# Softmax in an attention layer: the maxima subtracted on VectorE, one exponential for four heads on ScalarE

## The chip, the cores and the metric

The kernel runs on one core of a Trainium2 chip. The metric is the device time of one execution in microseconds (us). The engines are TensorE (PE in the profile, PEld for its weight loads), VectorE (DVE), ScalarE (ACT), GpSimd (POOL) and SyncE (SP).

## What is computed

Two layers, each an attention over a context of 128 rows and a mixture of eight experts, on 32 batches of 128 rows of 256 numbers:

```python
x = x + jnp.tanh(g_xattn[0]) * _L0_xattn_ref(_layernorm(x), ctx_1024, ctx_1024, ...)
x = x + jnp.tanh(g_ffn[0]) * _L0_ffn_ref(_layernorm(x), ...)
x = x + jnp.tanh(g_xattn[1]) * _L1_xattn_ref(_layernorm(x), ctx_1024, ctx_1024, mask, ...)
x = x + jnp.tanh(g_ffn[1]) * _L1_ffn_ref(_layernorm(x), ...)
```

The attention has 16 heads of 16 numbers; the second layer adds a mask to the scores:

```python
scores = jnp.einsum('bhqd,bhkd->bhqk', q, k) / jnp.sqrt(jnp.float32(D_K))
attn = jax.nn.softmax(scores, axis=-1)
out = jnp.einsum('bhqk,bhkd->bhqd', attn, v)
```

## The kernel before, in words

Each layer has an attention stage and an expert stage, one after the other. The change lies in the attention stages.

An attention stage works through 128 **units**: a batch and four of its heads, so four units per batch. The order is written out by hand. Every engine runs one loop over **steps** s, and in step s does its part of the units and batches that are due then; what is due when stands in the loop as an offset. Engines wait for each other by counters only (`w.wait_ge`), and each works through its own list in order. Sixteen steps are four batches, a **group**; the work for a group (layer norm, transposes of its rows, query, key and value projections, and the routing of an earlier group's rows to the experts) is spread over the 16 steps, so steps differ. Steps are named here by their place in the 16.

A unit i goes through these places:
- TensorE, step i - 4: scores of 128 query rows by 4 heads x 128 keys, into one of three PSUM banks (`SB_[i % 3]`, `ps0` to `ps2`), by three matmuls (lines 420 to 422; in the second layer a fourth, line 518, adds the mask). The query weights are scaled negatively, so the scores are negated and the largest weight belongs to the minimum.
- VectorE, step i - 3: the minimum of each head's 128 scores (line 1153) into `mx`. It is the first thing that VectorE does in a step.
- ScalarE, step i - 2: exp(minimum - score), one activation for each head, since the bias is one number per row and head (line 743), from the bank into one of three buffers of weights, `PB[:, i % 3]` (in `U`, `U3` with its number).
- TensorE, step i: four transposes of `PB` (line 500, counter `m_t`), into one of two banks `PTB` (`ps3`, `ps4`), which the transposes of the outputs (line 525) take turns with. It is the first thing that TensorE does in a step; the scores of unit i + 4 follow.
- ScalarE, step i: a copy of the transposed weights into `PT` (line 750). TensorE then multiplies them with the values (line 488), two units at a time, in the even steps.

Every fourth step (3, 7, 11, 15) VectorE goes on behind the reduction with the reciprocal (line 1157) and the normalisation (line 1163) of the batch whose outputs TensorE transposed a step earlier. The transposes of the next step (line 500 in steps 4, 8, 12, 0) need the bank that line 1163 reads. Behind that, VectorE has the low parts of projected rows (lines 916, 922 or 924, 932 or 934), statistics (1079, 1083, 1227, 1231), layer norm (1093, steps 4 and 5, for TensorE's transposes, line 435, in steps 6 and 7), and the routing's small operations. Line 916 in step 8 is what the query projection of that step waits for.

TensorE in step s may write the scores of unit s + 4 when the bank's unit s + 1 is done with.

Of the kernel before, what the change touches and what calls it, by code (L numbers as in the profile page):

```python
# [10 lines left out]
ACT = mybir.ActivationFunctionType  # L11
ALU = mybir.AluOpType
AX = mybir.AxisListType
# [133 lines left out]
def program(nc, A):  # L147
    ctx = ExitStack()
    with ctx:  # L149
# [3 lines left out]
        def mark(name, keys, step=1):  # L153
            return Mark(ctx.enter_context(nc.semaphore(name)), keys, step)
# [38 lines left out]
        mx = sb("mx", [128, 4, 4])  # L193
# [40 lines left out]
        PB = U3[:, 0:1536].rearrange("p (r h k) -> p r h k", r=3, h=4)  # L234
# [9 lines left out]
        SB_, PTB, OB, BK, BO_, HBK, YB, XB = PS[0:3], PS[3:5], PS[5], PS[6], PS[7], PS[0:4], PS[4:6], PS[6:8]  # L244
# [8 lines left out]
        units = [(L, i) for L in LL for i in range(NU)]  # L253
# [35 lines left out]
        m_s, m_t, m_av = (mark(n, units) for n in ("m_s", "m_t", "m_av"))  # L289
# [1 line left out]
        m_o, a_o = mark("m_o", bats), mark("a_o", bats)  # L291
        m_ot, m_op = mark("m_ot", range(B)), mark("m_op", range(B))
        m_lt, m_lg, m_rk = mark("m_lt", prt2), mark("m_lg", prts), mark("m_rk", prts)
        v_mx, a_p, a_pt = (mark(n, units) for n in ("v_mx", "a_p", "a_pt"))
        a_xt, v_xt, a_q, v_q, a_k, v_k, a_v = (mark(n, gt2) for n in ("a_xt", "v_xt", "a_q", "v_q", "a_k", "v_k", "a_v"))
        a_ct, v_st1 = (mark(n, grps) for n in ("a_ct", "v_st1"))
        p_ct, v_ct = mark("p_ct", [k for k in grps if k[1]]), mark("v_ct", [(0, 0), (1, 0)])
# [194 lines left out]
        def pe_attention(e, w, L):  # L492
            pe_first(e, w, L)
            for s in range(FIRST, LAST):
                if 0 <= s < NU:
                    i, bank = s, pt_place["p", s]
                    w.wait_ge(*a_p[L, i])
                    turn_free(w, L, "p", i)
                    for h in range(4):
                        ins = e.transpose(bank[:, h * 128:(h + 1) * 128], PB[:, i % 3, h], ident)  # L500
                    ins.then_inc(*m_t(L, i))
                if 0 <= s + 4 < NU:
                    i = s + 4
                    b, m, z = i // 4, (i // 2) % 2, i % 2
                    g, j, bank = b // G, b % G, SB_[i % 3]
                    w.wait_ge(*v_q[L, g, 1])
                    if i < 2:
                        w.wait_ge(*a_v[L, 0, i])
                    w.wait_ge(*d_k[key_queue(L, b)][L, b, 7])
                    if i >= 3:  # L510
                        w.wait_ge(*a_p[L, i - 3])
                    js = slice(j * 128, j * 128 + 128)
                    kh, kl = (KX[:, b % 2, p, m, 4 * z:4 * z + 4, :].rearrange("p h k -> p (h k)") for p in range(2))
                    ins = three(e, bank[:, :], (QR[:, g % 2, 0, m, js], QR[:, g % 2, 1, m, js]), (kh, kl), True, L == 0)
                    if L == 1:
                        w.wait_ge(*v_mk[g])
                        w.wait_ge(*s_ir[0])
                        ins = e.matmul(bank[:, :], IR[:, :], MK[:, g % 2, j:j + 1, :].to_broadcast([128, 4, 128]), start=False, stop=True)
                    ins.then_inc(*m_s(L, i))
# [209 lines left out]
        def act_attention(e, w, L):  # L729
            act_first(e, w, L)  # L730
            for s in range(FIRST, LAST):
                if (b := bat(s, OC)) is not None:
                    w.wait_ge(*m_av[L, 4 * b + 3])
                    if b:
                        w.wait_ge(*m_o[L, b - 1])
                    e.activation(OS[:, :], OB[:, :], ACT.Copy).then_inc(*a_o(L, b))
                if 0 <= s + 2 < NU:
                    i = s + 2
                    w.wait_ge(*v_mx[L, i])
                    if i >= 3:  # L740
                        w.wait_ge(*m_t[L, i - 3])
                    for h in range(4):
                        ins = e.activation(PB[:, i % 3, h], SB_[i % 3][:, h * 128:(h + 1) * 128], ACT.Exp, bias=mx[:, i % 4, h:h + 1], scale=-1.0)  # L743
                    ins.then_inc(*a_p(L, i))
                if 0 <= s < NU:
                    i = s
                    w.wait_ge(*m_t[L, i])
                    if i >= 3:
                        w.wait_ge(*m_av[L, i - 3])
                    e.activation(PT[:, i % 3].rearrange("p h k -> p (h k)"), pt_place["p", i][:, :], ACT.Copy).then_inc(*a_pt(L, i))  # L750
                if (g := grp(s, -2)) is not None:
                    act_context(e, w, L, g)
                for at, take in ((X0, act_turn), (Q0, act_query), (K0, act_key), (V0, act_value)):
                    for n in range(2):
                        if (g := grp(s, at[n])) is not None:
                            take(e, w, L, g, n)
                if L == 0 and (b := bat(s, 8)) is not None:
                    w.wait_ge(*m_ot[b])
                    if b >= 2:
                        w.wait_ge(*m_op[b - 2])  # L760
                    e.activation(OT[:, b % 2, 0].rearrange("p t n -> p (t n)"), place[0, "ot", b][:, 0:256], ACT.Copy).then_inc(*a_ot(b))
                for p in PARTS:
                    k, g, js = (L,) + p.key, p.g, p.js
                    for t in range(2):
                        if s == p.lt[t]:
                            cs = slice(p.lo * 128, p.hi * 128)
                            w.wait_ge(*m_lt[k + (t,)])
                            if p.lo == 0 and g:
                                w.wait_ge(*m_lg[L, g - 1, 0])
                            e.activation(LT[:, t, cs], place[L, "lt", p.key, t][:, cs], ACT.Copy).then_inc(*a_lt(*k, t))  # L770
                    if s == p.lt[1]:
                        w.wait_ge(*v_xr[k])
                        if p.lo == 0 and 0 < g < NG - 1:
                            w.wait_ge(*d_sc[(g - 1) % 2][L, g - 1, 0, 1, G - 1])
                        e.activation(xr(g)[:, 1, js, 0:D], xr(g)[:, 0, js, 0:D], ACT.Copy).then_inc(*a_xr(*k))
                    if s == p.exp:
                        if L == 0:
                            w.wait_ge(*v_ga1[k])
                            e.activation(rt[:, 1, js, 0], rt[:, 0, js, 0], ACT.Exp).then_inc(*a_gx(*k))
                        else:  # L780
                            w.wait_ge(*v_ga1[k])
                            e.activation(rt[:, 3, js], rt[:, 1, js], ACT.Exp)
                            e.activation(rt[:, 6, js], rt[:, 4, js], ACT.Exp).then_inc(*a_gx(*k))
# [361 lines left out]
        def dve_attention(e, w, L):  # L1145
            dve_first(e, w, L)
            for s in range(FIRST, LAST):
                if 0 <= s + 3 < NU:
                    i = s + 3
                    w.wait_ge(*m_s[L, i])  # L1150
                    if i >= 4:
                        w.wait_ge(*a_p[L, i - 4])
                    e.tensor_reduce(mx[:, i % 4], SB_[i % 3][:, :].rearrange("p (h k) -> p h k", h=4), AX.X, ALU.min).then_inc(*v_mx(L, i))  # L1153
                if (b := bat(s, 7)) is not None:
                    w.wait_ge(*m_o[L, b])
                    o = pt_place["o", b][:, :].rearrange("p (h d) -> p h d", d=32)
# [512 lines left out]
```

## Time and profile before

| | us |
|---|---|
| median of 3 runs | 1687.52 |
| lowest, highest | 1686.19, 1691.3 |
| the profiled execution, first to last instruction (span) | 1689.9 |
| attention of the first layer, first to last reduction | 27.5 to 358.5 |
| attention of the second layer | 916.3 to 1259.3 |

The page prints the span of the profiled execution and no other time of it. A row of busy time by stretch gives, for each engine, the microseconds in which it executed something; a row of waits gives who sat idle until whom. Engine time that is not busy can be a wait for another engine, or the short gap between two dependent operations on the same engine.

### The profile page before, as it was taken

How to read it: one execution, taken by the hardware profiler on the slowest of the kernel's cores; microseconds unless marked ns; L12 is line 12 of the kernel's file. 1: busy time of each engine (PE TensorE's matmuls, PEld its weight loads, DVE VectorE, ACT ScalarE, POOL GpSimd, SP SyncE). 2: the span in 40 equal slices, each digit the busy share in tenths (PEclk: the TensorE clock that was granted, in tenths of full speed). 3: DMA queues.
4: the chain of work that ended last, by engine and by line, in shares of the span. 5: the costliest groups of instructions: out<-in, count | busy, mean ns of one | idle time of the engine just before them, and what ended most of it. 6: DMA issues, size and time to landing. Idle time of an engine off the chain costs nothing. (4 is left out here: it accounts for less than half of the span.)

```text
span 1689.9 us, 37219 instructions
## 1 busy us (share of the span) xinstructions
PE 1575.0 (93%) x12832; PEld 1424.2 (84%) x12832; DVE 1194.5 (71%) x2829; ACT 1232.1 (73%) x2859; POOL 826.4 (49%) x887
## 2 busy tenths in 40 slices
PE   7999999976999999999988999999984999999996
PEld 5788888865999999999986777777773899999996
DVE  5677777755777777777766788888857566766664
ACT  5888888853888888888863877777771577777774
POOL 3224444343556565656552113333323477777776
PEclk9999999987999999999998999999995999999999
DMA  3222222135877777778742223333232788788883
GB/s 110 54 50 75 75 76 76 51 95 148 261 235 235 224 230 228 232 226 236 225 141 78 72 82 104 107 104 104 62 90 77 200 225 242 222 230 231 226 233 99
DMA packets 208988, 256.56 MB, mean 152 GB/s; under 512 B 29555, under 2 KB 156788, under 8 KB 208800
## 3 DMA queue, kind: packets, MB, share of 16 engines
q1 hardware_dynamic: 185408, 217.95, 44.2%
q0 software_dynamic: 21120, 34.39, 7.9%
q10 hardware_dynamic: 2272, 1.85, 0.4%
q8 instruction: 102, 1.67, 0.4%
q14 instruction: 86, 0.70, 0.1%
HBM read 194.54 MB, written 45.74 MB: 142 GB/s over the span
## 5 line engine op out<-in xcount | busy, mean ns | idle before, releaser
L1276 POOL TENSOR_TENSOR KXR<-U,KXR 128x1024 fp32r<-128x1024 f32 (+1 forms) x156 | 355.2, 2277 | 276.9 <-ACT KXR L795 276.9
L420 PE MATMUL ps<-QR,KXR 128*128 128x256 f32 x1248 | 360.4, 289 | 0.8 <-DVE QR L1280 0.7
L422 PE MATMUL ps<-QR,KXR 128*128 128x256 f32 x1248 | 354.2, 284 | 0.0
L421 PE MATMUL ps<-QR,KXR 128*128 128x256 f32 x1248 | 354.0, 284 | 0.0
L795 ACT ACTIVATE KXR<-U 128x1024 fp32r<-128x1024 f32 (+1 forms) x312 | 287.4, 947 | 73.2 <-PE ps L422 49.4
L743 ACT ACTIVATE U<-ps,mx 128x128 f32<-128x128 f32 x1024 | 299.0, 405 | 20.3 <-DVE mx L1153 20.3
L420 PEld LDWEIGHTS ps<-QR,KXR 128*128 128x128 f32 x1248 | 240.6, 193 | 1.4 <-DVE QR L1280 1.3
L421 PEld LDWEIGHTS ps<-QR,KXR 128*128 128x128 f32 x1248 | 240.4, 193 | 0.0
L422 PEld LDWEIGHTS ps<-QR,KXR 128*128 128x128 f32 x1248 | 240.0, 192 | 0.0
L1153 DVE TENSOR_REDUCE mx<-ps 128x4 f32<-128x512 f32 x256 | 174.3, 684 | 69.3 <-PE ps L422 37.1
L1276 DVE TENSOR_TENSOR KXR<-U,KXR 128x1024 fp32r<-128x1024 f32 (+1 forms) x156 | 175.0, 1160 | 25.6 <-ACT KXR L795 25.5
L1403 POOL DMA_INDIRECT xs_scr<-XR,PI x112 | 109.8, 980 | 133.6 <-DVE PI L1060 104.6
L500 PE MATMUL ps<-cst,U 128*128 128x128 f32 x1024 | 163.5, 283 | 10.0 <-DVE U L1163 9.5
L750 ACT ACTIVATE U<-ps 128x512 f32<-128x512 f32 x256 | 166.5, 650 | 7.4 <-PE ps L500 7.4
L500 PEld LDWEIGHTS ps<-cst,U 128*128 128x128 f32 x1024 | 117.3, 143 | 48.1 <-issue 23.6
L821 ACT ACTIVATE U<-ps,b1s 128x256 f32<-128x256 f32 x312 | 130.4, 473 | 29.9 <-PE ps L422 29.9
L1307 DVE TENSOR_TENSOR PTR<-U,PTR 128x512 fp32r<-128x512 f32 x80 | 101.0, 1298 | 60.6 <-ACT PTR L832 60.6
L420 PE MATMUL ps<-KXR,PTR 128*128 128x256 f32 x480 | 136.1, 284 | 3.6 <-ACT U L810 1.5
L1307 DVE TENSOR_TENSOR WR<-U,WR 128x512 fp32r<-128x512 f32 x76 | 97.9, 1326 | 56.6 <-ACT WR L832 56.6
L421 PE MATMUL ps<-KXR,PTR 128*128 128x256 f32 x480 | 135.8, 283 | 0.0
L422 PE MATMUL ps<-KXR,PTR 128*128 128x256 f32 x480 | 135.8, 283 | 0.0
L1419 POOL DMA_INDIRECT out<-U,xi x78 | 121.1, 1552 | 20.0 <-issue 19.7
(206 smaller groups left out, 4043.3 us busy)
## 6 DMA issues: line engine op xcount, KB each, us to landing
U<-in_wpack SPq DMA_DIRECT2D x234, 512.0 KB, 4.4
U<-in_wpack SPq DMA_DIRECT2D x78, 256.0 KB, 4.2
KXR<-U SPq DMA_DIRECT2D x504, 32.0 KB
U<-xs_scr SPq DMA_DIRECT2D x39, 258.0 KB, 4.5
U<-xs_scr SPq DMA_DIRECT2D x39, 257.0 KB, 4.7
U<-in_ctx_t SPq DMA_DIRECT2D x16, 512.0 KB, 5.7
U<-ys_scr SPq DMA_DIRECT2D x32, 256.0 KB, 3.4
XR<-in_L_ffn_b SPq DMA_DIRECT2D x39, 128.0 KB, 3.9
```

The source lines that it names most:

```text
L420: e.matmul(o, wh, xh, start=first, stop=False)
L421: e.matmul(o, wh, xl, start=False, stop=False)
L422: return e.matmul(o, wl, xh, start=False, stop=done)
L500: ins = e.transpose(bank[:, h * 128:(h + 1) * 128], PB[:, i % 3, h], ident)
L743: ins = e.activation(PB[:, i % 3, h], SB_[i % 3][:, h * 128:(h + 1) * 128], ACT.Exp, bias=mx[:, i % 4, h:h + 1], scale=-1.0)
L750: e.activation(PT[:, i % 3].rearrange("p h k -> p (h k)"), pt_place["p", i][:, :], ACT.Copy).then_inc(*a_pt(L, i))
L795: e.activation(w_cols(L, WH, n), w_raw(L, n), ACT.Copy).then_inc(*a_w[n](L, i))
L821: ins = e.activation(HB[:, r, f], HBK[q][:, z * 256:z * 256 + 256], ACT.Relu, bias=b1s[:, r, f:f + 1])
L1153: e.tensor_reduce(mx[:, i % 4], SB_[i % 3][:, :].rearrange("p (h k) -> p h k", h=4), AX.X, ALU.min).then_inc(*v_mx(L, i))
L1276: e.tensor_tensor(w_cols(L, WL, n), w_raw(L, n), hi, ALU.subtract).then_inc(*l_w[n](L, i))
L1307: ins = e.tensor_tensor(low[:, 2 * q:2 * q + 2], HB[:, i % 2, 2 * q:2 * q + 2], high[:, 2 * q:2 * q + 2], ALU.subtract)
L1419: ins = e.indirect_dma_start(ys_d[1], at, yo[:, r, a, :], None, bounds_check=T - 1, oob_is_err=False, compute_op=ALU.add)
```

## The change

VectorE gets a second operation behind each reduction: minimum - score for all four heads, 128x512, from the bank into the buffer of weights, the minima read with a step of zero over 128 columns. ScalarE then takes the exponential of the buffer in place, in one activation without a bias from memory. A new counter, `v_sb`, tells that the subtraction is done: ScalarE waits for it, and so does TensorE before it writes new scores into the bank. The wait for the buffer to be free (`m_t` of the unit three back) moves from ScalarE to VectorE, which also waits for its own reduction (`v_mx`) and no longer for the exponential four units back.

```diff
@@ pe_attention
                     if i >= 3:
-                        w.wait_ge(*a_p[L, i - 3])
+                        w.wait_ge(*v_sb[L, i - 3])
@@ act_attention
                     i = s + 2
-                    w.wait_ge(*v_mx[L, i])
-                    if i >= 3:
-                        w.wait_ge(*m_t[L, i - 3])
-                    for h in range(4):
-                        ins = e.activation(PB[:, i % 3, h], SB_[i % 3][:, h * 128:(h + 1) * 128], ACT.Exp, bias=mx[:, i % 4, h:h + 1], scale=-1.0)
-                    ins.then_inc(*a_p(L, i))
+                    w.wait_ge(*v_sb[L, i])
+                    flat = PB[:, i % 3].rearrange("p h k -> p (h k)")
+                    e.activation(flat, flat, ACT.Exp).then_inc(*a_p(L, i))
@@ dve_attention
                     w.wait_ge(*m_s[L, i])
-                    if i >= 4:
-                        w.wait_ge(*a_p[L, i - 4])
-                    e.tensor_reduce(mx[:, i % 4], SB_[i % 3][:, :].rearrange("p (h k) -> p h k", h=4), AX.X, ALU.min).then_inc(*v_mx(L, i))
+                    scores = SB_[i % 3][:, :].rearrange("p (h k) -> p h k", h=4)
+                    e.tensor_reduce(mx[:, i % 4], scores, AX.X, ALU.min).then_inc(*v_mx(L, i))
+                    if i >= 3:
+                        w.wait_ge(*m_t[L, i - 3])
+                    w.wait_ge(*v_mx[L, i])
+                    e.tensor_tensor(PB[:, i % 3], mx[:, i % 4, :, None].to_broadcast([128, 4, 128]), scores, ALU.subtract).then_inc(*v_sb(L, i))
```

Line numbers shift by up to three; line 1153 is the reduction before and the subtraction after.

VectorE in the first layer, step 3 of a middle group, before (the names in brackets are the counters that an operation waits for):

```order
L993 TENSOR_TENSOR rt<-m8 128x4
L1153 TENSOR_REDUCE mx<-ps1 128x4 [waits a_p,m_s]
L1157 RECIPROCAL rec<-ps3 128x16 [waits m_o]
L1163 TENSOR_TENSOR U4<-ps3,rec 128x256 [waits m_ot,v_c]
L950 SCALAR_TENSOR_TENSOR X<-ps7,th,X 128x256 [waits p_xb,m_op]
L965 COPY RK<-ps6 128x64 [waits m_rk]
```

And after:

```order
L990 TENSOR_TENSOR rt<-m8 128x4
L1149 TENSOR_REDUCE mx<-ps1 128x4 [waits m_s]
L1153 TENSOR_TENSOR U3<-mx,ps1 128x512 [waits v_mx,m_t]
L1157 RECIPROCAL rec<-ps3 128x16 [waits m_o]
L1163 TENSOR_TENSOR U4<-ps3,rec 128x256 [waits m_ot,v_c]
L947 SCALAR_TENSOR_TENSOR X<-ps7,th,X 128x256 [waits p_xb,m_op]
L962 COPY RK<-ps6 128x64 [waits m_rk]
```

The subtraction stands between the reduction and the normalisation, with a wait for this step's transposes.

VectorE in the second layer, steps 5 to 7 of a middle group, before:

```order
L1153 TENSOR_REDUCE mx<-ps1 128x4 [waits a_p,m_s]
L1093 TENSOR_SCALAR U2<-X,mv,rs 128x256 x2
L1153 TENSOR_REDUCE mx<-ps2 128x4 [waits a_p,m_s]
L1102 TENSOR_TENSOR MK<-U3,cst 128x512 [waits p_mf]
L1153 TENSOR_REDUCE mx<-ps0 128x4 [waits a_p,m_s]
L1157 RECIPROCAL rec<-ps4 128x16 [waits m_o]
L1163 TENSOR_TENSOR U4<-ps4,rec 128x256 [waits v_c]
L1167 SCALAR_TENSOR_TENSOR X<-U4,th,X 128x256 [waits v_on]
L916 TENSOR_TENSOR PTR<-ps6,PTR 128x512 [waits a_xt]
```

And after:

```order
L1149 TENSOR_REDUCE mx<-ps1 128x4 [waits m_s]
L1153 TENSOR_TENSOR U3<-mx,ps1 128x512 [waits v_mx,m_t]
L1090 TENSOR_SCALAR U2<-X,mv,rs 128x256 x2
L1149 TENSOR_REDUCE mx<-ps2 128x4 [waits m_s]
L1153 TENSOR_TENSOR U3<-mx,ps2 128x512 [waits v_mx,m_t]
L1099 TENSOR_TENSOR MK<-U3,cst 128x512 [waits p_mf]
L1149 TENSOR_REDUCE mx<-ps0 128x4 [waits m_s]
L1153 TENSOR_TENSOR U3<-mx,ps0 128x512 [waits v_mx,m_t]
L1157 RECIPROCAL rec<-ps4 128x16 [waits m_o]
L1163 TENSOR_TENSOR U4<-ps4,rec 128x256 [waits v_c]
L1167 SCALAR_TENSOR_TENSOR X<-U4,th,X 128x256 [waits v_on]
L913 TENSOR_TENSOR PTR<-ps6,PTR 128x512 [waits a_xt]
```

Three operations are added in a stretch of nine rows; the rest keeps its order.

ScalarE in the first layer, steps 8 and 9 of a group, before:

```order
L743 ACTIVATE U3<-ps0,mx 128x128 [waits v_mx]
L743 ACTIVATE U3<-ps0,mx 128x128 x3
L750 ACTIVATE U3<-ps4 128x512 [waits m_av,m_t]
L668 ACTIVATE QR<-ps7,bqk 128x512 [waits m_s,m_q]
L761 ACTIVATE OT<-ps6 128x256 [waits m_op,m_ot]
L736 ACTIVATE OS<-ps5 128x512 [waits m_o,m_av]
```

And after:

```order
L741 ACTIVATE U3<-U3 128x512 [waits v_sb]
L747 ACTIVATE U3<-ps4 128x512 [waits m_av,m_t]
L668 ACTIVATE QR<-ps7,bqk 128x512 [waits m_s,m_q]
L758 ACTIVATE OT<-ps6 128x256 [waits m_op,m_ot]
L736 ACTIVATE OS<-ps5 128x512 [waits m_o,m_av]
```

Four activations from the bank become one within the buffer.

## Rows read from the trace of the kernel before

**Rows 1.** The page's first section: busy us, share of the span, instructions.
```profile
PE 1575.0 (93%) x12832; PEld 1424.2 (84%) x12832; DVE 1194.5 (71%) x2829; ACT 1232.1 (73%) x2859; POOL 826.4 (49%) x887
```

**Rows 2.** Busy time by stretch: start:end, length, then each engine; the two stages.
```profile
core 0: us, PE busy (x) PEld busy (x) DVE busy (x) ACT busy (x) POOL busy (x), PEclk, DMA share, GB/s
27.46:358.50 331.04, 320.81 (x2795) 260.94 (x2793) 231.47 (x698) 275.64 (x781) 121.03 (x265) 1.00 0.26 70
916.26:1259.30 343.04, 323.37 (x2678) 255.81 (x2676) 275.15 (x818) 263.95 (x755) 105.21 (x242) 0.98 0.32 91
```

**Rows 3.** The same for one middle group of each layer, cut into stretches.
```profile
191.10:206.37 15.27, 15.27 (x138) 12.68 (x137) 10.08 (x38) 13.92 (x38) 3.06 (x2) 1.00 0.15 31
206.37:219.35 12.98, 12.52 (x120) 10.06 (x119) 11.90 (x41) 11.60 (x35) 7.50 (x18) 1.00 0.29 79
219.35:234.50 15.15, 14.78 (x121) 12.35 (x119) 9.52 (x24) 10.67 (x30) 7.68 (x20) 1.00 0.39 114
...
1085.75:1116.90 31.15, 28.71 (x229) 22.65 (x228) 29.70 (x100) 23.87 (x69) 10.64 (x20) 0.95 0.18 48
1117.00:1132.03 15.03, 15.03 (x130) 12.23 (x129) 9.06 (x22) 10.67 (x31) 5.44 (x17) 1.00 0.69 202
```

**Rows 4.** Timeline, second layer: start, length, engine, line, operation, idle before and releaser.
```profile
1103.25 0.68 DVE L1153 TENSOR_REDUCE mx<-ps 128x4 f32<-128x512 f32 x1
1103.85 0.25 DVE L1157 RECIPROCAL rec<-ps 128x16 f32<-128x16 f32 x1
1104.13 0.42 DVE L1163 TENSOR_TENSOR U<-ps,rec 128x256 f32<-128x256 f32 x1
...
1104.61 0.66 PE L500 MATMUL ps<-cst,U 128*128 128x128 f32 x4 [1.91 <-DVE U L1163]
```

**Rows 5.** Timeline, first layer, around steps 3 to 8 of one group.
```profile
209.07 0.42 DVE L1163 TENSOR_TENSOR U<-ps,rec 128x256 f32<-128x256 f32 x1
...
209.25 0.66 PE L500 MATMUL ps<-cst,U 128*128 128x128 f32 x4
...
216.12 0.63 PE L435 MATMUL ps<-cst,U 128*128 128x128 f32 x4 [0.44 <-DVE U L1093]
...
221.26 0.47 PE L420 MATMUL ps<-PTR,WR 128*128 128x512 f32 x1 [0.37 <-DVE PTR L916]
```

**Rows 6.** Groups by line and shape: count, busy us, mean ns, idle before.
```profile
L916 DVE TENSOR_TENSOR PTR<-ps,PTR 128x512 fp32r<-128x512 f32 x32 | 21.8, 685 | 6.1 <-ACT PTR L659 6.0
L1163 DVE TENSOR_TENSOR U<-ps,rec 128x256 f32<-128x256 f32 x64 | 27.2, 425 | 2.2
L922 DVE SCALAR_TENSOR_TENSOR QR<-ps,bqk,QR 128x512 fp32r<-128x512 f32 x16 | 12.0, 751 | 23.9 <-ACT QR L668 23.9
L1102 DVE TENSOR_TENSOR MK<-U,cst 128x512 fp32r<-128x512 f32 x8 | 5.4, 681 | 0.0
...
L736 ACT ACTIVATE OS<-ps 128x512 f32<-128x512 f32 x64 | 38.9, 609 | 9.0 <-PE ps L488 8.9
```

**Rows 7.** Busy time of line 1153 alone (VectorE) in the two full stretches.
```profile
206.37:219.35 12.98, 4.01 (x6) 1.00 0.29 79
1085.75:1116.90 31.15, 7.48 (x11) 0.95 0.18 48
```

**Rows 8.** Line 743: its group on the page, and who waited for it.
```profile
L743 ACT ACTIVATE U<-ps,mx 128x128 f32<-128x128 f32 x1024 | 299.0, 405 | 20.3 <-DVE mx L1153 20.3
...
  PEld ps L420: 7.0, 15
  PE ps L420: 3.8, 7
```

**Rows 9.** Busy time of TensorE and its granted clock (third number) by stretch.
```profile
1105.60:1108.40 2.80, 2.80 (x23) 0.50 0.21 42
```

**Rows 10.** Timeline of VectorE and GpSimd, second layer, step 15.
```profile
1089.56 2.60 DVE L1072 SCALAR_TENSOR_TENSOR X<-U,GT,X 128x256 f32<-128x256 f32 x1
...
1089.45 2.43 POOL L1351 TENSOR_TENSOR PTR<-U,PTR 128x1024 fp32r<-128x1024 f32 x1 [6.75 <-ACT PTR L653]
```

More of the change, by code:

```diff
@@ L293, in program @@
         m_lt, m_lg, m_rk = mark("m_lt", prt2), mark("m_lg", prts), mark("m_rk", prts)
-        v_mx, a_p, a_pt = (mark(n, units) for n in ("v_mx", "a_p", "a_pt"))
+        v_mx, v_sb, a_p, a_pt = (mark(n, units) for n in ("v_mx", "v_sb", "a_p", "a_pt"))
         a_xt, v_xt, a_q, v_q, a_k, v_k, a_v = (mark(n, gt2) for n in ("a_xt", "v_xt", "a_q", "v_q", "a_k", "v_k", "a_v"))
```

## The prediction

> **What bounds the kernel now.** I read five views, from the whole to the place. The page's first section gives the share of each engine in the span: TensorE 93%, VectorE 71%, ScalarE 73% [rows 1]. The change touches only the two attention stages, so I next read the busy time stage by stage. In the first layer's stage (331.04 us) TensorE is busy for 320.81, VectorE for 231.47, ScalarE for 275.64; in the second layer's (343.04 us) it is 323.37, 275.15 and 263.95 [rows 2]. Read as averages, TensorE is the bound and VectorE has 30% and 20% to spare. One group of 16 steps from the middle of each stage tells more. In the first layer VectorE is busy 11.90 of the 12.98 us from step 2 to step 7 and only 10.08 of 15.27 and 9.52 of 15.15 on either side. In the second it is busy 29.70 of the 31.15 us from step 14 to step 8 of the next round, and 9.06 of the other 15.03 [rows 3]. What is missing in the full stretches are gaps of some hundredths of a microsecond between dependent small operations, and at most one short wait. So VectorE is not an engine with 25% to spare: it is full for a third of each group in the first layer and for two thirds in the second, and idle in the rest, where the query, key and value projections keep TensorE busy without a break.
>
> The waits say that TensorE already feels the full stretches. In the second layer its transposes wait 1.91 us for line 1163, VectorE's normalisation one step earlier [rows 4]. In the first layer it waits 0.44 us for line 1093 (layer norm) and 0.37 us for line 916 (low part of the turned rows), both at the end of the full stretch [rows 5]. These are small, but they show that no slack is left between the two engines there: what makes VectorE later at these places makes TensorE later.
>
> **The price of a subtraction.** The trace has no instruction just like the new one: 128x512, scores from PSUM, four maxima each spread over 128 columns, result to SBUF. Line 916 is a TENSOR_TENSOR of the same size with one input in PSUM (685 ns), line 1163 one with a spread operand (425 ns for 256 columns), line 922 a heavier form (751 ns) [rows 6]. The nearest is 0.685. In the queue, a 0.68 us reduction that is followed by independent work holds VectorE for 0.60 (1103.25 to 1103.85); a dependent operation starts 0.03 after the end of the one before it (line 1157, 0.25 long, 1103.85; line 1163 at 1104.13) [rows 4]. So reduction and subtraction hold it for 0.68 + 0.03 + about 0.61 = 1.32 where the reduction held it for 0.60: **0.72 us per unit**. Bounds: 0.60, if the dependence costs nothing; 0.79, if the subtraction lasts as long as line 922. A gain is excluded here, since the reduction stays.
> The Trainium skill (Perfetto Trace Analysis, Optimizing Scalar/DVE Operations) puts the overhead of a VectorE operation that reads PSUM at about 125 ns, against about 60 ns for SBUF. By it 512 columns would cost an estimated 0.66 us, and 123 of them 81 us. The rows do not bear the difference out: line 1102 reads SBUF and takes 681 ns, line 916 reads PSUM and takes 685 [rows 6].
>
> **Part by part.** (1) *VectorE gets 256 subtractions*, 184 us at 0.72. Those in stretches where it idles cost nothing: there each group has 10 steps (first layer) or 5 (second), thus 7.2 and 3.6 us, against 10.8 and 6.0 us of idle time in the same rows [rows 3]. TensorE's projections hide them, and without this cover they would cost 0.72 each. Those in full stretches lie on the path: 6 reductions stand in the first layer's and 11 in the second's [rows 7]. I take five middle groups of each layer at the full count, 5 x (6 + 11) = 85, and the other three of each, the first two and the last, which lack part of the routing work that fills VectorE, at three quarters, 38: together 123. **123 x 0.72 = 89 us.** With 0.60 and 0.79 it is 74 and 97.
> (2) *VectorE gets a wait* before the subtraction, for the transposes of the unit three back, which TensorE does at the start of the same step. Queued behind it are, every fourth step, lines 1157 and 1163, for which the next transposes wait, and the low parts that the projections need. Where TensorE runs ahead it costs nothing, and a late VectorE lets it run ahead. The place where it is not: in the first layer TensorE transposes at 209.25 to 209.91, and line 1163 follows VectorE's reduction at 209.07 [rows 5]. After the change the subtraction can't start before 209.91 and line 1163 ends 0.68 + 0.03 + 0.25 + 0.03 + 0.42 later, at 211.3. By the count of subtractions alone it would be 209.49 + 2 x 0.72 = 210.9. The wait's 0.4 us is made up where TensorE must wait for line 1093 in any case; I take nothing, and 0.4 x 8 = 3 us for the range.
> (3) *ScalarE loses* four activations per unit, 299.0 us in 256 units, 1.17 us each, and gets one of 128x512, for which line 736 takes 609 ns [rows 6, 8]: some 0.56 us less per unit, 144 us in all. On the path there is little of it: all that TensorE waited for line 743, weight loads and matmuls together, is 10.8 us [rows 8]. I count nothing.
> (4) *The score bank is free earlier*: TensorE's next scores wait for the subtraction, no longer for the exponential behind it. That wait is within the same 10.8 us. The removed wait of the reduction (for the exponential four units back) never shows. TensorE's own list is unchanged.
>
> **The sum.** 1689.9 (span) + 89 = 1779. The page prints the span and not the time around it; the median of the runs is 2.4 below that span, so on its scale I predict 1687.5 + 89 = **1777 us**.
>
> **Rivals.**
> *A: the averages decide.* Three score banks and three weight buffers might let VectorE fall behind in the full stretch and catch up in the idle one. Then a group needs only its total. First layer: 11.5 + 31.5 = 43.0 in 43.4 us, no change. Second: 11.5 + 38.8 = 50.3 against 46.2, 4.1 us in five groups: 1687.5 + 21 = 1708. Against it stand the waits without slack [rows 4, 5]: line 1163 lies between TensorE's steps every fourth step, and banks don't help there. Chance 0.09.
> [...]
> *B: the clock.* In the second layer, after the 1.91 us in which TensorE did nothing, its granted clock reads 0.50 (1.2 GHz of its 2.4) for the 2.80 us from 1105.60 [rows 9], so 1.4 us of work at the full clock took twice that. The change makes several stalls of 1 to 4 us per group. If each group loses one such 1.4 us more on the path, 16 groups lose 22: 1687.5 + 89 + 22 = 1799. It decides if TensorE, once released, is what VectorE or the next projection waits for. In the second layer VectorE stays the later one, which speaks against it; the first layer's projections follow right behind its stalls, which speaks for it. Chance 0.15.
> *C: not slower.* ScalarE's relief is what counts: TensorE's waits for line 743 vanish (10.8 us), and the subtractions hide as the stage averages suggest: 1687.5 - 11 = 1677. It needs the full stretches to be waits in disguise, with VectorE held up by others. Within them rows 3 leave 1.1 and 1.5 us for all gaps and waits, which is against it. Chance 0.03.
> That the change doesn't do what it says is out: the order shows one subtraction behind each reduction and one activation for four.
>
> **How the numbers follow.** The forecast has 0.70; A 0.09, B 0.15, C 0.03, and 0.03 is left for more than all this. One term can go either way: once per group of the second layer line 1072 lasts 2.60 us beside GpSimd's line 1351 instead of about 0.48 [rows 10]; a shifted start can lose that overlap or add one, 2.1 us in 7 groups, 15 us. Low end: 74 - 15 - 4 of slack that I may have missed, 1687.5 + 55 = 1742. High end: 97 + 22 + 3 + half of 15, 1687.5 + 129 = 1816. It takes in B and leaves A, C and the rest out. A measurement of this kernel can tell about 0.3% (5 us) from no change. Faster by more: 0.03 (C); within: 0.03 (between C and A); slower: 0.94.
>
> **What would show it.** In the profile after: the subtraction at 0.68 to 0.70 us; VectorE about 184 us busier, ScalarE about 140 less; the first layer's stage some 31 us longer and the second's some 57; TensorE's waits for lines 1163, 1093 and 916 up from a dozen to tens of microseconds; the projections' stretches (from 219.35 and from 1117.0) as long as before. If the stages grow by 0 and 20, A is right; if the granted clock of the stages falls well below the 1.00 and 0.98 of rows 2 and the projections' stretches grow, B. I am wrong in the main if TensorE's waits for VectorE stay as they are while VectorE is busier, or if subtractions last well over 0.8 us.

## The result and the profile after

| | before | after |
|---|---|---|
| median of 4 runs each (us) | 1688.5 | 1837.9 |
| lowest, highest | 1686.2, 1691.3 | 1836.1, 1840.9 |
| span of the profiled execution | 1689.9 | 1835.1 |
| first layer's attention, first to last reduction | 330.3 | 409.4 |
| second layer's attention, first to last reduction | 343.9 | 413.3 |
| from the first layer's last reduction to the second's first | 556.9 | 557.2 |

The changed kernel takes 1.0885 times as long, interval [1.0863, 1.0906]: 149 us more. The prediction said slower, by 89, with 1816 as the upper end of the range; the time lies 22 us above that end and 61 above the forecast. All but a microsecond of it is in the two attention stages, 79 us in the first layer and 69 in the second. The stages are measured here from the start of the first reduction to the start of the last. (The second layer's first reduction starts at 914.7 us in the kernel before, not at 916.3 as in the table ahead of the prediction; nothing above hangs on it.)

The first section of the page after (busy us, share of the span, instructions) against [rows 1]:

```profile
PE 1617.9 (88%) x12832; PEld 1445.4 (79%) x12832; DVE 1354.9 (74%) x3085; ACT 1117.1 (61%) x2091; POOL 826.7 (45%) x887
```

VectorE is 160 us busier and ScalarE 115 less. The groups by line (count, busy us and mean ns of one, then the idle time of the engine before them and who ended it), against [rows 6, 8]. Line 1153 is now the subtraction, 1149 the reduction, 741 the exponential:

```profile
L1153 DVE TENSOR_TENSOR U<-mx,ps 128x512 f32<-128x512 f32 x256 | 176.1, 688 | 137.5 <-PE ps L500 120.5 <-DVE mx L1149 1.1
L1149 DVE TENSOR_REDUCE mx<-ps 128x4 f32<-128x512 f32 x256 | 172.5, 674 | 1.6 <-PE ps L518 1.3 <-PE ps L422 0.3
L500 PE MATMUL ps<-cst,U 128*128 128x128 f32 x1024 | 170.8, 292 | 53.9 <-ACT U L741 46.9 <-DVE U L1163 5.9 <-ACT U L747 1.0
L741 ACT ACTIVATE U<-U 128x512 f32<-128x512 f32 x256 | 160.4, 627 | 78.6 <-DVE U L1153 75.8
```

The subtraction takes 688 ns and the exponential of four heads 627 ns, as foreseen. Unforeseen is the first row's idle time: VectorE sat 120.5 us in front of the subtraction, waiting for the transposes of line 500. The waits (engine, what it was about to write, line, for whom: total us, times, longest):

```profile
DVE U L1153 <- PE ps L500: 120.5, 97, 2.9
...
PE ps L435 <- DVE U L1090: 32.5, 14, 4.4
...
PE ps L420 <- DVE PTR L913: 19.5, 16, 1.7
```

The first row is VectorE in front of the subtraction, 97 times. The exponential comes behind the subtraction: ScalarE waits for it 75.8 us (the fourth row of the groups), and TensorE's transposes wait for the exponential 46.9 (the third row). Before, TensorE's transposes hardly waited for ScalarE's exponentials at all (0.4 us of line 500's weight loads in the whole run). Lines 1090 and 913 are the layer norm and the low part that were lines 1093 and 916. TensorE waits for them 32.5 and 19.5 us, against 9.2 and 7.0 before. The prediction named line 1163 first; the transposes now wait for it 5.9 us in all (the third row of the groups).

Busy time by stretch, columns as in [rows 2]: the two stages, and the same pieces of a middle group as in [rows 3], cut at the same units' reductions:

```profile
26.30:436.40 410.10, 344.63 (x2795) 269.62 (x2793) 312.48 (x824) 218.73 (x400) 120.71 (x265) 0.95 0.21 56
992.90:1406.80 413.90, 347.44 (x2684) 271.52 (x2682) 355.68 (x946) 208.01 (x376) 106.83 (x242) 0.93 0.27 75
```

```profile
226.90:244.60 17.70, 15.77 (x116) 12.41 (x116) 12.88 (x45) 10.18 (x18) 3.10 (x3) 0.90 0.10 21
244.60:264.79 20.19, 14.33 (x118) 10.54 (x117) 16.87 (x47) 8.79 (x17) 10.47 (x21) 0.92 0.27 80
264.79:282.97 18.18, 16.67 (x143) 13.52 (x142) 12.39 (x29) 10.12 (x20) 4.64 (x17) 1.00 0.25 67
1202.08:1241.58 39.50, 29.30 (x220) 22.71 (x219) 36.91 (x112) 17.89 (x33) 13.47 (x22) 0.91 0.18 49
1241.58:1258.07 16.49, 16.49 (x140) 13.56 (x139) 11.77 (x27) 9.72 (x18) 3.09 (x15) 1.00 0.56 158
```

The first layer's pieces were 15.27, 12.98 and 15.15 us and are now 17.70, 20.19 and 18.18: the full stretch grew by 7.2, and the two pieces of projections, in which VectorE idles, grew by 2.4 and 3.0. In the second layer the full stretch (31.15) grew by 8.4 and the other (15.03) by 1.5. The subtractions alone were to lengthen the full stretches, and only those. In two of the three pieces with idle time the granted clock is 1.00, as before, so in these the clock is not what made them longer.

The timeline shows how a stretch with idle time grows. The end of step 8 and step 9 of a middle group, first layer, VectorE and TensorE (start, length, engine, line, operation, idle before it and releaser):

```profile
266.28 0.68 DVE L913 TENSOR_TENSOR PTR<-ps,PTR 128x512 fp32r<-128x512 f32 x1
...
267.11 0.47 PE L420 MATMUL ps<-PTR,WR 128*128 128x512 f32 x1 [0.77 <-DVE PTR L913]
...
267.43 0.66 DVE L1149 TENSOR_REDUCE mx<-ps 128x4 f32<-128x512 f32 x1
...
269.46 0.66 PE L500 MATMUL ps<-cst,U 128*128 128x128 f32 x4
...
270.15 0.69 DVE L1153 TENSOR_TENSOR U<-mx,ps 128x512 f32<-128x512 f32 x1 [2.06 <-PE ps L500]
...
270.76 0.74 DVE L919 SCALAR_TENSOR_TENSOR QR<-ps,bqk,QR 128x512 fp32r<-128x512 f32 x1
...
271.56 0.50 PE L420 MATMUL ps<-PTR,WR 128*128 128x512 f32 x1 [0.74 <-DVE QR L919]
```

VectorE ends step 9's reduction at 268.09 (267.43 + 0.66) and then stands for 2.06 us: its next operation, the subtraction, needs the transposes at 269.46, and TensorE does those behind the projection that began at 267.11 and behind the values' product. Line 919, the low part of the projected rows, is queued behind the subtraction, and the next projection (271.56) waits for line 919. Projection, transposes, subtraction, low part, next projection: one after the other. From projection to projection it takes 4.45 us (271.56 - 267.11). The same step before, where the low part is line 922:

```profile
223.61 0.66 PE L500 MATMUL ps<-cst,U 128*128 128x128 f32 x4
223.64 0.75 DVE L922 SCALAR_TENSOR_TENSOR QR<-ps,bqk,QR 128x512 fp32r<-128x512 f32 x1 [1.39 <-ACT QR L668]
...
224.80 0.39 PE L420 MATMUL ps<-PTR,WR 128*128 128x512 f32 x1
```

There the low part runs beside the transposes, the projection doesn't wait, and from the projection at 221.26 [rows 5] to this one it is 3.54 us.

### The profile page after: what moved, and what is told of

It is laid out like the page before. It is cut to its first block and busy times, and to the rows that moved or that the text cites. A ratio compares the mean times of both kernels' runs of the same rounds, so it can differ in the third digit from the quotient of the medians.

```text
span 1835.1 us, 36893 instructions
## 1 busy us (share of the span) xinstructions
PE 1617.9 (88%) x12832; PEld 1445.4 (79%) x12832; DVE 1354.9 (74%) x3085; ACT 1117.1 (61%) x2091; POOL 826.7 (45%) x887
## 5 line engine op out<-in xcount | busy, mean ns | idle before, releaser
L1153 DVE TENSOR_TENSOR U<-mx,ps 128x512 f32<-128x512 f32 x256 | 176.1, 688 | 137.5 <-PE ps L500 120.5
L500 PE MATMUL ps<-cst,U 128*128 128x128 f32 x1024 | 170.8, 292 | 53.9 <-ACT U L741 46.9
L741 ACT ACTIVATE U<-U 128x512 f32<-128x512 f32 x256 | 160.4, 627 | 78.6 <-DVE U L1153 75.8
L1276 DVE TENSOR_TENSOR KXR<-U,KXR 128x1024 fp32r<-128x1024 f32 (+1 forms) x156 | 177.4, 1175 | 26.1 <-ACT KXR L792 26.0
L747 ACT ACTIVATE U<-ps 128x512 f32<-128x512 f32 x256 | 151.4, 591 | 66.6 <-PE ps L500 66.2
```

Source lines behind the costliest of these rows:

```text
L741: e.activation(flat, flat, ACT.Exp).then_inc(*a_p(L, i))
L1153: e.tensor_tensor(PB[:, i % 3], mx[:, i % 4, :, None].to_broadcast([128, 4, 128]), scores, ALU.subtract).then_inc(*v_sb(L, i))
L1276: e.tensor_tensor(w_cols(L, WL, n), w_raw(L, n), hi, ALU.subtract).then_inc(*l_w[n](L, i))
```

## The experiments

Two theories stood against each other for the missing 61 us. **W**: it is the wait that moved into VectorE's list, which the prediction took at nothing. **V**: the wait is a symptom; the added work of VectorE costs that much more than 0.72 us a subtraction, in the full stretches or in the others too. The clock (rival B of the prediction) stood beside them. All ratios are against the kernel before, run beside them.

**The wait taken away (e1_four).** A fourth buffer of weights; the subtraction then waits for transposes that TensorE did a step earlier. To make room for it, the second layer's mask is computed in place, and the load of the next mask waits for a later operation; e2_work, e6_idle and e8_full share this. e6_idle comes out within 3.5 us of the kernel before, so it costs little. The rest is as in the changed kernel.

```diff
...
+        P4 = U3[:, 3584:4096].rearrange("p (h k) -> p h k", h=4)
+        PBS = [PB[:, 0], PB[:, 1], PB[:, 2], P4]
...
-                    if i >= 3:
-                        w.wait_ge(*m_t[L, i - 3])
+                    if i >= 4:
+                        w.wait_ge(*m_t[L, i - 4])
                     w.wait_ge(*v_mx[L, i])
-                    e.tensor_tensor(PB[:, i % 3], mx[:, i % 4, :, None].to_broadcast([128, 4, 128]), scores, ALU.subtract).then_inc(*v_sb(L, i))
+                    e.tensor_tensor(PBS[i % 4], mx[:, i % 4, :, None].to_broadcast([128, 4, 128]), scores, ALU.subtract).then_inc(*v_sb(L, i))
...
```

> The changed kernel with a fourth buffer of weights (the second layer's mask is computed in place to make room), so that the subtraction waits for the transposes of the unit four back, which TensorE did a step earlier. Theory W (the wait that moved into VectorE's queue costs what the prediction missed, about 60 of the 150 us, because in the steps with a projection it ties each VectorE step to the end of TensorE's step before): 1777 us, 1765 to 1790, and VectorE's wait before the subtraction falls from 120 us to under 30. Theory V (the work of the subtraction alone costs 150 us, since hardly any of it finds idle time): 1830 to 1840.

Measured: 1775.45 us, 1.0516 [1.0499, 1.0533]: 87 us over the kernel before and 62 under the changed one. The group of the subtraction (line 1155 here; lines are two further down) no longer names a releaser:

```profile
L1155 DVE TENSOR_TENSOR U<-mx,ps 128x512 f32<-128x512 f32 x256 | 176.0, 688 | 26.1
```

The 26.1 us over 256 of them are 0.10 each, the gap behind the reduction that it depends on. The same step as above, TensorE and VectorE:

```profile
245.28 0.47 PE L422 MATMUL ps<-PTR,WR 128*128 128x512 f32 x1 [0.39 <-DVE PTR L915]
...
245.60 0.66 DVE L1151 TENSOR_REDUCE mx<-ps 128x4 f32<-128x512 f32 x1
...
246.36 0.69 DVE L1155 TENSOR_TENSOR U<-mx,ps 128x512 f32<-128x512 f32 x1
...
247.63 0.66 PE L502 MATMUL ps<-cst,U 128*128 128x128 f32 x4
247.66 0.75 DVE L921 SCALAR_TENSOR_TENSOR QR<-ps,bqk,QR 128x512 fp32r<-128x512 f32 x1 [0.62 <-ACT QR L670]
...
248.83 0.40 PE L422 MATMUL ps<-PTR,WR 128*128 128x512 f32 x1
```

The subtraction (246.36) now runs while TensorE projects, the low part (line 921, 247.66) runs beside the transposes (line 502), and from projection to projection it takes 248.83 - 245.28 = 3.55 us instead of 4.45. By pieces of a middle group:

```profile
208.24:223.29 15.05, 15.05 (x138) 12.65 (x136) 13.28 (x44) 11.23 (x21) 3.11 (x3) 1.00 0.15 31
223.29:243.05 19.76, 15.51 (x120) 11.97 (x119) 17.11 (x48) 8.83 (x17) 10.57 (x21) 0.84 0.26 81
243.05:258.59 15.54, 15.15 (x121) 12.65 (x119) 12.75 (x29) 8.63 (x17) 4.55 (x17) 0.99 0.26 74
1152.41:1189.95 37.54, 29.63 (x228) 23.04 (x227) 34.94 (x113) 18.68 (x34) 13.38 (x22) 0.91 0.20 53
1189.95:1205.22 15.27, 15.27 (x132) 12.47 (x131) 12.35 (x27) 8.72 (x16) 3.10 (x15) 1.00 0.59 166
```

The projections' pieces are back to 15.05, 15.54 and 15.27, within 0.4 of [rows 3]; the full stretches keep 6.8 and 6.4 us more. W holds and V falls. W is not the whole of the 62 us, though: some 10 of them, in the second layer's full stretches, are another term (step (1) below).

**The work without the exchange (e2_work).** The kernel before, with the subtraction into a spare buffer that nobody reads; ScalarE keeps its four activations and waits for the subtraction.

```diff
...
                     e.tensor_reduce(mx[:, i % 4], SB_[i % 3][:, :].rearrange("p (h k) -> p h k", h=4), AX.X, ALU.min).then_inc(*v_mx(L, i))
+                    w.wait_ge(*v_mx[L, i])
+                    e.tensor_tensor(P4, mx[:, i % 4, :, None].to_broadcast([128, 4, 128]), SB_[i % 3][:, :].rearrange("p (h k) -> p h k", h=4), ALU.subtract).then_inc(*v_sb(L, i))
...
```

> The kernel before with the subtraction added into a spare buffer that nobody reads; the four exponentials stay, still read the scores, and wait for the subtraction. VectorE waits for nothing new. It measures the added work and the longer chain of a unit without the buffer wait and without ScalarE's relief. Theory W: 1777 to 1785 us. Theory V: 1830 or more.

Measured: 1771.74 us, 1.0500 [1.0478, 1.0521], 83 us; 5 us under the range expected by W, and far from V's. It is within 4 us of e1_four, though ScalarE is as busy as before (1235.7 us; 1114.7 in e1_four). So VectorE's work explains e1_four, and ScalarE's relief hardly shows.

**The wait without the work (e3_wait).** The kernel before, with VectorE waiting for the transposes behind its reduction, and nothing else.

```diff
                     e.tensor_reduce(mx[:, i % 4], SB_[i % 3][:, :].rearrange("p (h k) -> p h k", h=4), AX.X, ALU.min).then_inc(*v_mx(L, i))
+                    if i >= 3:
+                        w.wait_ge(*m_t[L, i - 3])
```

> The kernel before with the wait alone: VectorE waits behind each reduction for the transposes of the unit three back, and subtracts nothing. Theory W: the wait alone costs a large part of what was missed, 20 to 50 us: 1708 to 1738. Theory V: the wait costs nothing by itself, 1685 to 1693.

Measured: 1723.18 us, 1.0211 [1.0191, 1.0232], 35 us for a wait that computes nothing. The first layer's stage grows by 29.5 us, half of it (15.0) in its full stretches, and the second's by 4.3. Its largest wait on VectorE (line 1159 is the reciprocal, the first operation behind the wait every fourth step; in other steps the idle time stands at other lines):

```profile
DVE rec L1159 <- PE ps L500: 79.3, 53, 3.0
```

Wait alone 35 and work alone 83 make 118; the change costs 149. Some 10 of the missing 31 are the term of step (1) below, which both these kernels are without and the changed one has. Where wait and work are both there, the subtraction's own 0.69 us also lies in the chain between the transposes and the low part. That this accounts for the rest is argued, not shown.

**ScalarE's relief alone (e4_shared).** The kernel before, with one minimum for all four heads of a row, and so one activation with one bias for each row; VectorE has no more to do than before.

```diff
-                    for h in range(4):
-                        ins = e.activation(PB[:, i % 3, h], SB_[i % 3][:, h * 128:(h + 1) * 128], ACT.Exp, bias=mx[:, i % 4, h:h + 1], scale=-1.0)
-                    ins.then_inc(*a_p(L, i))
+                    e.activation(PB[:, i % 3].rearrange("p h k -> p (h k)"), SB_[i % 3][:, :], ACT.Exp, bias=mx[:, i % 4, 0:1], scale=-1.0).then_inc(*a_p(L, i))
...
-                    e.tensor_reduce(mx[:, i % 4], SB_[i % 3][:, :].rearrange("p (h k) -> p h k", h=4), AX.X, ALU.min).then_inc(*v_mx(L, i))
+                    e.tensor_reduce(mx[:, i % 4, 0:1], SB_[i % 3][:, :], AX.X, ALU.min).then_inc(*v_mx(L, i))
```

> The kernel before with one maximum over all four heads of a row instead of one for each (any shift that is the same for all keys gives the same softmax), so that one exponential of 128x512 with one bias per row replaces four, and VectorE does no more than before. It measures ScalarE's relief alone. Both theories: at most the 10.8 us that TensorE waited for the exponentials, 1677 to 1688. If ScalarE's relief were worth more than that, the changed kernel would have lost more on VectorE than 150 us.

Measured: 1682.99 us, 0.9965 [0.9951, 0.9978]: 5.5 us faster than before. The activation's group:

```profile
L742 ACT ACTIVATE U<-ps,mx 128x512 f32<-128x512 f32 x256 | 175.7, 687 | 36.0 <-DVE mx L1151 35.9
```

175.7 us in place of 299.0 [rows 8], so 123 us less work on ScalarE give 5.5. It beats both kernels, at a price in range of numbers: a head whose scores lie far under those of its three neighbours is computed against their extreme.

**The subtraction one unit later (e5_later).** The changed kernel with its three buffers; VectorE subtracts unit s + 2 ahead of the reduction of unit s + 3, so the subtraction follows a reduction of a whole step earlier.

```diff
             for s in range(FIRST, LAST):
+                if 0 <= s + 2 < NU:
+                    i = s + 2
+                    if i >= 3:
+                        w.wait_ge(*m_t[L, i - 3])
+                    w.wait_ge(*v_mx[L, i])
+                    e.tensor_tensor(PB[:, i % 3], mx[:, i % 4, :, None].to_broadcast([128, 4, 128]), SB_[i % 3][:, :].rearrange("p (h k) -> p h k", h=4), ALU.subtract).then_inc(*v_sb(L, i))
                 if 0 <= s + 3 < NU:
...
-                    if i >= 3:
-                        w.wait_ge(*m_t[L, i - 3])
-                    w.wait_ge(*v_mx[L, i])
-                    e.tensor_tensor(PB[:, i % 3], mx[:, i % 4, :, None].to_broadcast([128, 4, 128]), scores, ALU.subtract).then_inc(*v_sb(L, i))
```

> The changed kernel with three buffers, but with each subtraction one step later in VectorE's list: it stands ahead of the next unit's reduction, and the transposes that it waits for are those at the start of TensorE's step before. If it is the place of the wait that cost the 62 us between the changed kernel and the one with four buffers, it is gone here too: 1770 to 1790. If it is the buffer itself (held from subtraction to transposes, whatever the order), the time stays above 1815.

Measured: 1754.63 us, 1.0403 [1.0386, 1.0421]: 66 us over the kernel before, 83 under the changed one, 21 under e1_four and 15 under the range expected. So it is the place of the wait that counts, and not the number of buffers; that the time would fall below e1_four's was not foreseen. The wait for the transposes shrinks from 120.5 to

```profile
DVE U L1150 <- PE ps L500: 8.1, 22, 1.0
```

since the transposes in question are now a step old. And the subtraction is cheaper. First e5_later's timeline of VectorE, then e1_four's, both in the second layer:

```profile
1142.17 0.67 DVE L1150 TENSOR_TENSOR U<-mx,ps 128x512 f32<-128x512 f32 x1
1142.76 0.68 DVE L1155 TENSOR_REDUCE mx<-ps 128x4 f32<-128x512 f32 x1
1143.36 0.68 DVE L931 TENSOR_TENSOR U<-ps,U 128x512 fp32r<-128x512 f32 x1
```

```profile
1159.32 0.66 DVE L1151 TENSOR_REDUCE mx<-ps 128x4 f32<-128x512 f32 x1
1160.08 0.69 DVE L1155 TENSOR_TENSOR U<-mx,ps 128x512 f32<-128x512 f32 x1
...
1171.75 0.68 DVE L1151 TENSOR_REDUCE mx<-ps 128x4 f32<-128x512 f32 x1
1172.54 0.69 DVE L1155 TENSOR_TENSOR U<-mx,ps 128x512 f32<-128x512 f32 x1
```

Where nothing in the row depends on the operation in front of it, they follow each other in 0.59 and 0.60 us. Where the subtraction needs the reduction's result, it starts 0.76 to 0.79 us after the reduction's start. Over the 123 subtractions that the prediction counts as lying on the path, 0.17 to 0.20 us each would be 21 to 25 us, which is an estimate.

**The idle stretches alone, and the full ones alone (e6_idle, e8_full).** Four buffers as in e1_four; VectorE subtracts only for the units whose reduction lies in a stretch that the prediction called idle (120 units), all others go the old way. e8_full is the complement (136 units).

```diff
+        def on_dve(L, i):
+            return ((i - 3) % 16 in (9, 10, 11, 12, 13)) if L else ((i - 3) % 16 not in (2, 3, 4, 5, 6, 7))
...
+                    if on_dve(L, i):
+                        w.wait_ge(*v_sb[L, i])
+                        flat = PBS[i % 4].rearrange("p h k -> p (h k)")
+                        e.activation(flat, flat, ACT.Exp).then_inc(*a_p(L, i))
+                    else:
...
```

> Four buffers of weights; subtraction and single exponential only for the units whose VectorE step lies where VectorE idles (10 of 16 steps in the first layer, 5 in the second, 120 units), the four exponentials with a bias for the others. If the idle stretches hide a subtraction, as the prediction's first term says: 1685 to 1700 us. If a subtraction costs its 0.72 us wherever it stands: about 1770. If it costs its share of the 87 us: 1729.

> The complement: four buffers, subtraction and single exponential only for the 136 units of the full stretches. If only these cost: 1765 to 1780 us, as with all 256. If a subtraction costs its share of the 87 us wherever it stands: 1735.

Measured: e6_idle 1692.00 us, 1.0024 [1.0013, 1.0035]; e8_full 1774.31 us, 1.0513 [1.0496, 1.0531]. So 120 subtractions cost 3.5 us, 0.03 each, and 136 cost 86 us, 0.63 each. The two stages of e6_idle, columns as in [rows 2]:

```profile
26.30:358.90 332.60, 319.27 (x2795) 260.53 (x2793) 281.90 (x776) 238.70 (x544) 121.11 (x265) 1.00 0.26 69
918.40:1261.40 343.00, 320.78 (x2684) 254.23 (x2682) 299.55 (x858) 247.84 (x640) 104.81 (x242) 1.00 0.32 91
```

VectorE is busy 50 us longer in the first layer and 24 in the second, and the stages are 1.6 us longer and not longer at all. Cut at the reductions, e6_idle's idle stretches are 3.5 us longer in all, again 0.03 for each subtraction.

## Why the prediction was right and wrong

**What bounds the kernel: right.** VectorE's full stretches set the price and its idle ones don't: 0.63 us against 0.03 for each subtraction. Read by stage averages, VectorE had room for all of them (rival A, 1708); it fell. The Trainium skill (Perfetto Trace Analysis, Optimization Strategy) says that the most-contended engine can change between regimes of one kernel and that gaps are to be sought within each; these runs agree, down to regimes of 13 us.

**Step (1), the subtractions: right in kind, near in the sum by luck.** Forecast 89 us, measured 87 (e1_four) and 83 (e2_work), with errors that cancel. By layer it was 31 and 57 by forecast and 39 and 50 in e1_four, and in the pieces four things show.
The price was 0.79 and not 0.72 (0.79 was the forecast's upper bound, there for another reason): the gap behind the reduction is 0.10 and not 0.03, the value taken from lines 1157 and 1163 [rows 4]. 123 x 0.79 = 97.
The second layer lost an overlap that had made VectorE slow: line 1072, 2.60 us once per group beside GpSimd's line 1351 [rows 10], which the prediction named as a term of either sign. It is the first of a pair of operations of the same kind. The line before, then the same in e1_four (there line 1071), then the second of the pair in the changed kernel (line 1071 of that file):

```profile
L1072 DVE SCALAR_TENSOR_TENSOR X<-U,GT,X 128x256 f32<-128x256 f32 x32 | 26.8, 837 | 0.2 <-DMA U<-ys_scr 0.2
```

```profile
L1071 DVE SCALAR_TENSOR_TENSOR X<-U,GT,X 128x256 f32<-128x256 f32 x32 | 16.9, 528 | 0.0
```

```profile
L1071 DVE SCALAR_TENSOR_TENSOR X<-U,GT,X 128x256 f32<-128x256 f32 x32 | 27.5, 860 | 1.1
```

In e1_four 10 us of VectorE's time come back, some 2 per middle group. With it the second layer's full stretch adds up: 11 x 0.79 - 2.1 = 6.6, measured 6.4. The changed kernel keeps the overlap, now with the pair's second operation:

```profile
1203.71 2.48 POOL L1351 TENSOR_TENSOR PTR<-U,PTR 128x1024 fp32r<-128x1024 f32 x1 [3.87 <-ACT PTR L653]
...
1203.98 2.48 DVE L1071 SCALAR_TENSOR_TENSOR X<-U,GT,X 128x256 f32<-128x256 f32 x1
```

Both operations of the pair together take 42.3 us before, 44.5 in the changed kernel and 34.6 in e1_four. The full stretch of the second layer shows it: 39.50 us against 37.54, with VectorE busy 36.91 against 34.94. So 10 of the 62 us between these two kernels are this term and not the wait, and by this reading the subtractions of the changed kernel itself cost some 97, the upper bound of the forecast. This is read from the rows; no run takes the wait away and keeps the overlap. In e2_work, e3_wait and the runs that follow them it is gone as well (31 to 33 us for the pair).
The first layer paid for the clock. In e1_four TensorE waited 3.60 us for the layer norm. Its granted clock then was 0.50 (1.2 GHz of 2.4) for 4.7 us, its operations took about twice as long (four transposes 1.12 us in place of 0.60), and VectorE waited 1.50 us for scores that came late:

```profile
237.30 1.09 PE L437 MATMUL ps<-cst,U 128*128 128x128 f32 x4 [3.60 <-DVE U L1092]
...
240.61 1.12 PE L502 MATMUL ps<-cst,U 128*128 128x128 f32 x4
...
243.05 0.69 DVE L1151 TENSOR_REDUCE mx<-ps 128x4 f32<-128x512 f32 x1 [1.50 <-PE ps L424]
```

Busy time of TensorE and its granted clock (third number), as in [rows 9]:

```profile
237.30:242.00 4.70, 4.70 (x32) 0.50 0.24 86
```

The whole stretch has a granted clock of 0.84 in the pieces above, against 1.00 before [rows 3]. 6 x 0.79 + 1.5 = 6.2, measured 6.8. This is the mechanism of rival B, and the forecast had it at nothing.
The outer groups were counted too high. The first two and the last full stretch of the first layer grew by 1.4 to 2.1 us in e1_four and not by the 3.2 that three quarters of the count give; the five in the middle grew by 5.7 to 6.8 and not by 4.3.
The changed kernel has more of the clock's loss: TensorE is busy 1617.9 us against 1575.0 before and 1595.9 in e1_four for the same matmuls. How much of these 43 us lies on the path no run tells apart. e1_four has 21 of them and still comes out near the forecast's 89, and the 22 that the changed kernel has beyond it are far under 62. So the clock is a part of what the subtractions cost and of what the wait costs, and can't explain the missing 61 by itself.

**Step (2), the wait: this is the step that failed.** The prediction listed what is queued behind the wait, low parts included, and then took the wait at nothing, since "where TensorE runs ahead it costs nothing". It costs some 50 us: taking it away saves 62 (1837.9 - 1775.5), 40 in the first layer's stage and 19 in the second's, and 10 of the second's are the overlap of step (1). With the 97 of the subtractions this makes the 149. The prediction looked for the cost at step 3, in a full stretch, where TensorE waits for VectorE anyway, and found 0.4 us. Cut at the same reductions, the changed kernel's idle stretches are 33 us longer than e1_four's in the first layer and 7 in the second, its full ones 9 and 12, and in the 12 stands the overlap. So most of it arose in the idle stretches, where TensorE is the later engine and VectorE stands for up to 2.9 us in front of the subtraction: in the two idle pieces of the first layer's middle group TensorE waits 3.4 us for VectorE, and 0.4 before and in e1_four. There the prediction had counted VectorE's idle time as cover. But before, VectorE did its low part while TensorE transposed (223.64 beside 223.61), out of the bank that the projection had just filled. After, the low part is queued behind an operation that needs this step's transposes, which TensorE does behind its own projection. So VectorE's idle time there was a wait, and not free for other work. The bound of 0.4 x 8 = 3 us took the wait's price in one place for its price in all, and it was too low for the full stretches as well: the wait alone (e3_wait) lengthens those of the first layer by 15.0 us.

**Step (3), ScalarE's relief: right.** 10.8 us were the most that it could give, and nothing was counted; alone it gives 5.5, part of which may be the overlap of step (1), which e4_shared lost too.

**Step (4): right**, as far as seen. TensorE's scores hardly wait for their bank: line 420 with KXR and QR waits 2.4 us for line 1153 in all, and its weight loads 2.6 (from the groups by line).

**Rivals.** A and C fell. B's mechanism is there, but not as the main cost. The rival that was missing is the serial chain projection, transposes, subtraction, low part. Its beginning stood in the rows of before: in [rows 5] the projection at 221.26 waits for line 916. The prediction put this row at the end of the full stretch; by [rows 3] it lies 1.9 us inside the idle one that follows, and so shows that TensorE waits for VectorE there too. Had the working asked what line 916 and the other low parts, six in each group, would wait for behind the moved wait, it would have met this chain.

**The signs to watch.** Subtraction 688 ns (0.68 to 0.70 foreseen), VectorE +160 (184), ScalarE -115 (140), stages +79 and +69 (31 and 57). "The projections' stretches as long as before" was the sign that broke, and it pointed at the cause.

## What to carry to other kernels

A wait that moves to another engine stops everything behind it in that engine's list, so its price is to be worked out in every kind of stretch, the idle ones too: go from the wait to what is queued behind it, and on to the first operation of the bounding engine that needs one of those. Here the idle time of VectorE covered added work, but not an added wait for the engine that bounds. When an operation must be added to a full engine, put it a step behind what it depends on: here that was worth 0.17 to 0.20 us each, and it took most of the wait away as well. And when an experiment takes one cost away, compare the bounding engine's busy time too: here 10 us of the difference were an overlap that had moved.

## What the runs showed of the hardware

The subtraction of 128x512 on VectorE, which depends on the reduction in front of it, starts about 0.10 us after that one's end; operations of the same size that don't depend on the one in front start 0.08 before its end. From start to start it is 0.76 to 0.79 against 0.59 us. The Trainium skill (VectorE: DVE Perf Modes, The DRAIN you can't avoid) states that a semaphore between successive VectorE operations costs nothing extra, measured on copies. The rows of e1_four and e5_later differ by 0.17 to 0.20 us, and for these forms the measurement decides.

A wait of 3.60 us on TensorE was followed by operations at about half speed (1.12 us for four transposes, 0.60 otherwise), with a granted clock of 0.50 in the 4.7 us behind it. Here the stall cost the time of the wait, and then more in the work behind it.

VectorE's SCALAR_TENSOR_TENSOR of 128x256 takes 2.48 us beside GpSimd's TENSOR_TENSOR of 128x1024 (changed kernel, 1203.98) and 2.60 before [rows 10]; the mean of 528 ns in e1_four, where they are mostly apart, shows what it takes otherwise.
